# Early-fusion transformer layer: two patch embeddings moved ahead of the first scores, and the class row carried by the text transfer

## The reference

```python
# x (8, 3, 112, 112), txt (8, 128, 192)
patches = ...                                  # 49 patches of 16 x 16 x 3 = 768 numbers per image
embeds = einsum('bsp,pd->bsd', patches, W) + b + pos     # 49 rows of 192
h = concatenate([cls_embedding, embeds, txt])  # 1 + 49 + 128 = 178 rows per batch
# attention, 12 heads, queries and keys both xn * W_qk[head], values xn - mean(wte, axis=0)
xn = layernorm(layernorm(h)) * ln_w
out = softmax(causal(Q @ Q.T / sqrt(192))) @ (xn - avg_wte)
h = h + (out / position) @ W_o.T               # wte: 50257 x 192, read once for its mean
# 16 routed experts and one shared one, hidden size 128, then the residual
h = h + ffn(layernorm(h))
```

## Time and profile before

| | before |
|---|---|
| median of three executions | 447.61 us |
| lowest, highest | 445.42, 449.06 us |
| the profiled execution | 447.82 us |
| its span in the trace | 445.7 us |
| mean granted TensorE clock | 0.996 |
| TensorE busy | 434.3 us (97%) |
| VectorE busy | 277.3 us (62%) |
| ScalarE busy | 187.2 us (42%) |
| GpSimd busy | 68.3 us (15%) |
| DMA | 63.61 MB, mean 143 GB/s |

### The profile page before, as it was taken

The page is one execution under the profiler, slowest core; times in us unless marked ns, Lnnn a source line. Parts: engine busy times, 40 slices in busy tenths (PEclk is TensorE's granted clock), DMA queues, the critical chain, the costliest instruction groups (busy, mean ns, idle before and its releaser), DMA issues.

```text
span 445.7 us, 7188 instructions
## 1 busy us (share of the span) xinstructions
PE 434.3 (97%) x2572; PEld 378.3 (85%) x2572; DVE 277.3 (62%) x924; ACT 187.2 (42%) x565; POOL 68.3 (15%) x93
## 2 busy tenths in 40 slices
PE   8899999999999899999999999999999999999996
PEld 8687689877898667987779999999999999999995
DVE  5899865487654787447957855488553474433433
ACT  1766864447644466624532045633113412112111
POOL 4032122122212311210004114221002000000000
PEclk9999999999999999999989999999999999999999
DMA  5969999999999999997530052121332222322210
GB/s 175 295 245 211 213 213 213 213 213 215 213 214 213 214 213 213 214 214 190 209 121 2 1 220 76 50 67 49 89 91 63 63 69 60 97 68 69 64 42 35
DMA packets 20997, 63.61 MB, mean 143 GB/s; under 512 B 2572, under 2 KB 10836, under 8 KB 20578
## 3 DMA queue, kind: packets, MB, share of 16 engines
q0 software_dynamic: 7552, 39.39, 41.8%
q1 hardware_dynamic: 12546, 22.78, 17.3%
q10 hardware_dynamic: 864, 1.00, 0.7%
HBM read 61.88 MB, written 1.27 MB: 142 GB/s over the span
## 4 chain that ended last, share of the span: by engine, by line
PE 50%; DMA 44%; DVE 2%; issue 2%; SPq 1%; ACT 1%; POOL 1%; ACTq 0%; DVEq 0%
DMA area_w<-in_L_attn_wte_dram 39%; PE bank L927 15%; PE bank L898 5%; PE bank L897 5%; PE bank L895 5%; PE bank L896 5%; PE bank L894 5%; PE bank L810 3%; DMA woT<-in_L_attn_W_o_dram 3%; DMA lnw<-in_L_attn_ln_w_dram 1%; PE bank L757 1%; PE bank L921 1%; PE bank L783 1%; PE bank L748 1%; PE bank L782 1%
## 5 line engine op out<-in xcount | busy, mean ns | idle before, releaser
L810 PE MATMUL bank<-woT,area_o 128*128 128x192 f32 (+1 forms) x432 | 72.3, 327 | 0.0
L810 PEld LDWEIGHTS bank<-woT,area_o 128*128 128x128 f32 (+1 forms) x432 | 69.8, 182 | 0.6 <-issue 0.6
L521 ACT ACTIVATE pm<-pm,nmax 128x128 f32<-128x128 f32 x96 | 37.4, 390 | 72.9 <-DVE nmax L1031 72.9
L1128 DVE TENSOR_TENSOR area_b<-area_b,area_w 128x484 f32<-128x484 f32 (+1 forms) x36 | 24.1, 668 | 51.7 <-ACT area_b L594 50.4
L435 POOL DMA_DIRECT2D area_w<-in_L_attn_wte_dram x26 | 31.1, 1196 | 129.9 <-DMA area_w<-in_L_attn_wte_dram 129.9
L594 ACT ACTIVATE area_b<-bank,area_k 128x484 f32<-128x484 f32 (+1 forms) x24 | 15.8, 657 | 59.8 <-PE bank L898 59.8
L757 PE MATMUL bank<-pT,xn 128*128 128x356 f32 x96 | 39.7, 495 | 0.0
L544 ACT ACTIVATE area_b<-xb,w 64x192 f32<-64x192 f32 x96 | 38.1, 444 | 0.8
L894 PE MATMUL bank<-area_w_r,area_o_r 128*128 128x484 f32 (+1 forms) x84 | 37.4, 445 | 0.0
L927 PE MATMUL bank<-area_k,area_b 128*128 128x192 f32 (+1 forms) x192 | 35.3, 326 | 0.0
L927 PEld LDWEIGHTS bank<-area_k,area_b 128*128 128x128 f32 (+1 forms) x192 | 31.6, 182 | 0.9
(11 more groups left out here) (221 smaller groups left out, 916.6 us busy)
## 6 DMA issues: line engine op xcount, KB each, us to landing
area_w<-in_L_attn_wte_dram POOLq DMA_DIRECT2D x28, 1344.0 KB, 12.7
area_w<-gate_rows SPq DMA_DIRECT2D x24, 242.0 KB, 3.1
area_k<-in_experts_dram SPq DMA_DIRECT2D x8, 353.0 KB, 5.5
area_w<-gate_rows SPq DMA_DIRECT2D x12, 228.0 KB, 3.2
area_a<-in_experts_dram SPq DMA_DIRECT2D x6, 353.0 KB, 5.8
area_b<-gate_rows SPq DMA_DIRECT2D x8, 242.0 KB, 3.2
woT<-in_L_attn_W_o_dram SPq DMA_DIRECT2D x1, 1728.0 KB, 12.8
area_o<-in_x_dram SPq DMA_DIRECT2D x4, 384.0 KB, 5.8
```

Of the source, the lines that this page charges most:

```text
L521: act.activation(pm[:, sl, n, :], pm[:, sl, n, :], ACT.Exp, scale=-1.0, bias=nmax[:, sl, n:n + 1], accum_out=psums[:, sl, n:n + 1])
L810: last = pe.matmul(o, oT[:, c, at:at + n], woT[:, c, :], start=(c == 0), stop=(c == NCH - 1))
L1128: dve.tensor_tensor(sil[:, n % 2, 0:w], sil[:, n % 2, 0:w], wbc[m % RING][:, 0:w], ALU.mult).then_inc(weighted, 1)
```

## The change

- The class row is laid in DRAM ahead of each batch's text rows, so the text tensor has 129 rows. The first text transfer of each group then covers partitions 49 to 127, 79 rows, in place of 78. The transfer of the class row alone is gone, and VectorE's first wait is for 32 in place of 48.
- SP waits for the embedding weights alone (`s_tokw`) and then sends the patches of pairs 1 and 2; the wait for `s_small` comes behind them, and the one for `s_pos` is gone.
- `keep_awake(9)` becomes `keep_awake(2)` and `embed(1)`; `keep_awake(3)` ahead of the first scores becomes `embed(2)`. Both embeddings are gone from their later places.

```diff
--- before.py
+++ after.py
@@ -34,11 +34,12 @@
         self.n += 1
 
 
-def early_fusion_kernel(nc, x, txt, tok_W, tok_b, tok_pos, tok_cls, ln_w, W_qk, W_o, wte,
+def early_fusion_kernel(nc, x, txt, tok_W, tok_b, tok_pos, ln_w, W_qk, W_o, wte,
                         gate_w, gate_b, bias, experts, bdown, rows, out):
     PAIRS, _, KX, _ = x.shape
     B = 2 * PAIRS
     NTXT, _, E = txt.shape
+    NTXT -= 1
     NPOS = 49
     NIMG = 1 + NPOS
     S = NIMG + NTXT
@@ -320,22 +321,21 @@
             TM = P - NIMG
 
             def text_in(n, b0, b1):
-                sp.dma_start(hin[NIMG:P, b0:b1, 0, :], txt[0:TM, b0:b1, :]).then_inc(s_text[n], 16)
+                sp.dma_start(hin[NPOS:P, b0:b1, 0, :], txt[0:TM + 1, b0:b1, :]).then_inc(s_text[n], 16)
                 sp.wait_ge(s_zero, n + 1)
-                sp.dma_start(hin[0:TAIL, b0:b1, 1, :], txt[TM:NTXT, b0:b1, :]).then_inc(s_text[n], 16)
+                sp.dma_start(hin[0:TAIL, b0:b1, 1, :], txt[TM + 1:NTXT + 1, b0:b1, :]).then_inc(s_text[n], 16)
 
             sp.dma_start(ximg[:, 0], x[0]).then_inc(s_x[0], 16)
             text_in(0, 0, 2)
-            sp.dma_start(hin[NIMG - 1:NIMG, :, 0, :], tok_cls[0].rearrange("a (c e) -> a c e", c=1)
-                         .broadcast_to([1, B, E])).then_inc(s_text[0], 16)
-            sp.wait_ge(s_pos, 32)
+            sp.wait_ge(s_tokw, 16)
+            for i in range(1, 3):
+                sp.dma_start(ximg[:, i], x[i]).then_inc(s_x[i], 16)
             sp.wait_ge(s_small, 32)
-            sp.dma_start(ximg[:, 1], x[1]).then_inc(s_x[1], 16)
             text_in(1, 2, B)
-            for i in range(2, PAIRS):
+            for i in range(3, PAIRS):
                 sp.dma_start(ximg[:, i], x[i]).then_inc(s_x[i], 16)
             for k in range(2):
-                sp.dma_start(htail[TAIL * k:TAIL * k + TAIL, :, :], txt[TM:NTXT, k::2, :]).then_inc(s_text[1], 16)
+                sp.dma_start(htail[TAIL * k:TAIL * k + TAIL, :, :], txt[TM + 1:NTXT + 1, k::2, :]).then_inc(s_text[1], 16)
             sp.dma_start(woT[:], W_o).then_inc(s_wo, 16)
             sp.dma_start(gwa[:], gate_w[0:P, :]).then_inc(s_small2, 16)
             sp.dma_start(gwb[:], gate_w[P:2 * P, :]).then_inc(s_small2, 16)
@@ -672,7 +672,8 @@
             keep_awake(7)
             pe.wait_ge(s_tokw, 16)
             embed(0)
-            keep_awake(9)
+            keep_awake(2)
+            embed(1)
             pe.wait_ge(s_const, 1)
 
             def turn_in(b, bt, i):
@@ -812,12 +813,11 @@
                     last.then_inc(wo_done, 1)
 
             turn_in(0, 0, 0)
-            keep_awake(3)
+            embed(2)
             pe.wait_ge(s_pad, 1)
             queries_in(0, 0)
             scores(0, 0)
             turn_in(1, 1, 0)
-            embed(1)
 
             def mean():
 
@@ -848,8 +848,6 @@
                         project(i - 1, 2)
                     if u >= 1:
                         mix(u - 1, U + u - 1, i)
-                    if i == 0 and u == 0:
-                        embed(2)
                     if i == 0 and u == 1:
                         pe.wait_ge(xnT_ready, 4)
                         embed(3)
@@ -1170,7 +1168,7 @@
                 rows = slice(64 * half, 64 * half + NPOS)
                 return dve.tensor_tensor(hin[0:NPOS, half, 0, :], emb_bank[0][rows, 0:E], postab[rows, :], ALU.add)
 
-            dve.wait_ge(s_text[0], 48)
+            dve.wait_ge(s_text[0], 32)
             variance((1, 3), OPENING[0])
             dve.wait_ge(s_pos, 32)
             link(dve.tensor_tensor(postab[:], postab[:], tokb[:], ALU.add))
@@ -1387,7 +1385,7 @@
             finish(NG - 1)
 
 
-_INS = ['x', 'txt', 'L0_tok_W', 'L0_tok_b', 'L0_tok_positions', 'L0_tok_cls_embedding', 'L0_attn_ln_w', 'L0_attn_W_qk',
+_INS = ['x', 'txt', 'L0_tok_W', 'L0_tok_b', 'L0_tok_positions', 'L0_attn_ln_w', 'L0_attn_W_qk',
         'L0_attn_W_o', 'L0_attn_wte', 'L0_ffn_gate_w', 'L0_ffn_gate_b', 'L0_ffn_bias', 'experts', 'bdown']
 _OUTS = [((128, 12, 192), 'float32')]
 
@@ -1461,6 +1459,7 @@
     given = {name: _np.asarray(a) for name, a in inputs.items()}
     ffn = {name[len('L0_ffn_'):]: a for name, a in given.items() if name.startswith('L0_ffn_')}
     given['experts'] = _experts(*[ffn[n] for n in ('Wu', 'bu', 'Wg', 'bg', 'Wd', 'sWu', 'sbu', 'sWg', 'sbg', 'sWd')])
+    given['txt'] = _np.concatenate([_np.broadcast_to(given['L0_tok_cls_embedding'], (8, 1, 192)), given['txt']], axis=1)
     given['bdown'] = _np.zeros((P, 192), _np.float32)
     given['bdown'][0:17] = _np.concatenate([ffn['bd'], ffn['sbd'][None]])
     given['L0_ffn_gate_w'] = _np.concatenate([ffn['gate_w'], _np.zeros((64, 16), _np.float32)])
```

## The result

| | before | after |
|---|---|---|
| median of 5 runs | 446.82 us (445.42 to 449.06) | 462.59 us (460.78 to 463.22) |
| ratio, 95% interval | | 1.036 (1.033 to 1.039) |
| profiled execution, its span | 447.8, 445.7 us | 462.9, 460.9 us |

The changed kernel is slower by 3.6%. Between the two profiled executions lie 15.1 us, between the two spans 15.2 us. The forecast was 470 us in a range of 457 to 483.

A forecast was written before the change was run, and what follows sets the result against it. The prediction took the wte stream, started by woT's landing, as the bound. woT's delay, 4.2 + 18.8 - 2 = 21 us, plus 1 us for the clock, gave 447.8 + 21 + 1 = 469.8, so 470 us, range 457 to 483.

The forecast's parts named there:

- The bound is the stream that woT's landing starts: 28 back-to-back wte transfers, started by woT's landing, set the clock until 206 us; woT and stream end 21 us later.
- 79 rows go to one engine: 79 is prime, so one DMA engine carries all 158 and 474 text packets of the two groups; chance in order 0.84.
- Price of a packet, 43 ns: Time of one 768-byte text packet on its DMA engine, taken as 43 ns between bounds of 31.5 and 71.5.
- the forecast's 2.0 for contention: 2 us taken off woT's delay because the other DMA engines are out of work after some 22 us.
- How the delay comes about: SP's queue drains as before, and woT waits behind the text on the one engine, landing at about 46 us.
- First statistics at 14.4 with a wait of 8: VectorE's first statistics move from 7.92 to 14.4 us, behind the first group's text, with a wait of 8 us.
- TensorE's own path: The remaining text lands 13 us later, 15 with contention, less than the stream's 21; the six between are waited.
- One us for the clock: 1 us added for TensorE's lowered clock behind an idle stretch of several us before 227 us.
- Embeddings for zeros -0.7 us: Embeddings moved into the place of products of zeros take 0.7 us off TensorE's path.
- patches earlier -2.1 us: The second pair's patches are issued 2.1 us earlier, moving everything behind them on SP's queue, woT included, 2.1 us earlier.
- The first rival: The 79-row text is spread over many engines all the same; 446.1 us, 1.7 under the profiled execution, chance 0.11.
- The rival of woT not held: One engine carries the text but woT is served beside it, so only the text's landings count; 453.4 us, chance 0.05.

The follow-up runs named there:

- e1: The changed kernel with each 79-row text transfer cut into 1 and 78 rows; 445.5 us, ratio 0.998 to the kernel before.
- e4: The changed kernel with each 79-row text transfer cut into 15 and 64 rows; 445.6 us, ratio 0.997 to the kernel before.
- e5: The changed kernel with each 79-row text transfer cut into 5 and 74 rows; 451.5 us, ratio 1.013 to the kernel before.
- e6: The changed kernel with each 79-row text transfer cut into 3 and 76 rows; 447.3 us, ratio 1.002 to the kernel before.
- e12: The changed kernel, 79-row transfers kept, with woT issued ahead of the second group's text; 464.1 us, ratio 1.039 to the kernel before.
- e7: The changed kernel with 79 rows kept only in the first group, the second group's cut into 15 and 64; 451.3 us, ratio 1.014 to before.
- e8: The changed kernel with 79 rows kept only in the second group, the first group's cut into 15 and 64; 459.5 us, ratio 1.030 to before.
- e3: The kernel before with only the moved embeddings and SP's new order, class row still its own transfer, 78 text rows; 444.8 us, ratio 0.996.
- e9: e3 with GpSimd's rstd moved from behind the second to behind the fourth transfer of wte; 444.6 us, ratio 0.997 to the kernel before.
- e11: The kernel before with only SP's new order, embeddings and products of zeros in their old places; 444.3 us, ratio 0.997.
- e2: The kernel before with only the class row laid with the text (79-row transfers), embeddings and SP's order as before; 461.9 us, ratio 1.036.

## Why the prediction was right, step by step

- **The bound is the stream that woT's landing starts.** Right. Landing +15.4, sum +15.2, span +15.2. The end was reached through the last `rstd` in the stream's order (+16.2) and not through the last transfer.
- **79 rows go to one engine.** Right, and shown: 2914 packets, as forecast to the packet; a share of 0.07; e1, e4, e5 and e6 bring the time back in the order of the engine counts.
- **Price of a packet, 43 ns.** This is the term that was mis-sized. A lone engine took 34 ns. The 43 came from a stretch in which many engines worked at once, and it was worked out from the share, which makes 1.1 engines of a lone one: by the same way the lone engine has 0.070 x 16 x 5 us over 147 packets, 38 ns. So of the 9 ns too much about 4 lie in the way of counting and 5 in the crowded stretch. The lower bound, 31.5 ns, was nearer. e12's 86 ns is above the upper bound, but only while something else has the engine too.
- **The sum with 34 ns.** 146 x 0.034 = 5.0 for the first group, less 2.1 for the earlier issue, 438 x 0.034 = 14.9 for the second, less the forecast's 2.0 for contention, is 15.8, and 15.4 was measured. That it comes so close is partly luck, since the terms by themselves are off. By the stream's start all but the 79 rows brought 1.6 us (before to e4), the first group cost 3.7 (e7) and the second 13.7 (e8), and together they cost 0.4 less than that: -1.6 + 3.7 + 13.7 - 0.4 = 15.4. Each of these is one trace, and e3 and e9, with the same instructions on SP, start the stream at 21.44 and 23.22, so a term is known to 1 or 2 us only. The forecast also wasn't the same sum at its ends as in its middle: the sum with 31.5 ns takes off 2.4 for contention, the one with 71.5 ns nothing, and neither adds the 1 us for the clock.
- **How the delay comes about.** In part wrong. The prediction had SP issue everything on time, and woT wait on the slow engine behind the text. It was SP's issue of the next transfer that was held, for 17.22 us, and with it the patches, `htail` and woT for *all* engines. The sum came out alike because woT needs its last part either way. But the sign named for it (a share of 0.06 between 25 and 40 us) wasn't there: the share stood at 0.07 from 12 to 26.6 us, and from 28 to 40 it was 0.76, since what SP had been kept from issuing ran then on all engines.
- **First statistics at 14.4 with a wait of 8, from 43 ns a packet.** 13.12 and 6.97; with 34 ns the same sum gives 13.1.
- **TensorE's own path 13 to 15 us later, under the stream's 21.** It was 8.8, under 15.2. The order of the two was right, the sizes follow the packet price, and the difference of 6 was waited, as said. Of the two places named for the waiting, L1300 and `rs`, only the second was right: 0.78 us at the sum, not several, and 9.02 in one wait for `rs`.
- **One us for the clock.** It did not come. The forecast wanted an idle stretch of several us ahead of 227, and TensorE waited for nothing from 190 to 222 us. It did stand still for 4.46 us ahead of an embedding and for 6.69 ahead of the second row below, and its granted clock was lower behind both (0.62 from 14 to 16 us, 0.50 from 108 to 112), but both lie under the stream.

```profile
14.12 3.90 PE L664 MATMUL bank<-wtok,area_o 128*128 128x192 f32 x12 [4.46 <-DMA area_o<-in_x_dram]
...
109.20 1.12 PE L723 MATMUL bank<-ident,pm 128*128 128x128 f32 x4 [6.69 <-DVE pm L1038]
```

- **Embeddings for zeros -0.7 us, patches earlier -2.1 us.** The second is seen: e11 starts the stream at 21.85 instead of 25.17, 3.3 earlier, and has the sum 2.9 earlier; the medians are 1.6 apart (444.34 and 445.90). But in the change itself the 79 rows left little of it: 0.55 us between e2 and the change. The first rival, the text spread over many engines, was to be 1.7 us under the kernel before; e1 and e4, which spread it, are 1.0 and 0.9 under it. The 0.7 us isn't seen at all; e11 and e3 can't be told apart.
- **The rival of woT not held.** 453.4 us was its number. e12, which comes nearest to it, put woT ahead of the text and took 464.1: the rival counted the text's landing without what stands behind it on GpSimd, and without the sharing of the engine.

So the forecast (469.8 before rounding) was 7.2 us high in a sum whose bound and engine count held, while the way in which the delay comes about was wrong in part. 438 + 146 packets at 9 ns too much are 5.3 us, and the clock, which cost nothing, 1.0. The 34 ns sum is still 0.4 over what was measured, and the last half microsecond is between 447.8 + 15.4 = 463.2 and the median.

## What to carry to other kernels

Before adding a row to a transfer, look at what divides the new row count. One more row took a transfer from 13 engines to 1, and cutting the same bytes in two (1 + 78, 15 + 64) gave the whole loss back. The packet counts of a queue bear on the number of engines already in the trace before: what is left over after the data packets is the sum of the engines of its transfers, and two windows with different transfers in them, as the earlier trace rows, pin down the single ones. And when a transfer is made slow, ask what stands behind it in each order it is part of: here woT on SP's queue, and behind that, once woT was taken out of its way, the wte stream behind `rstd` on GpSimd.

## What the runs showed of the hardware

- One DMA engine alone took a 768-byte packet every 34 ns, 23 GB/s (147 packets in 5 us, the change); two engines took 118 in 2 us, 45 GB/s (e5). Beside the stream of wte the text got one packet through every 86 ns (81 in 7 us, e12).
- The issue that followed a one-engine transfer in the queue was held: 4.93 us behind 158 packets, 17.22, 15.71 and 14.96 us behind 474 (the change, e2, e8), 29.62 us where the engine was shared (e12), 5.66 behind a transfer on two engines (e5), 1.63 behind one on four (e6). Behind 78 rows on 13 engines it took 0.41 (e1). What in the queue holds it, no run shows. The prediction had no such term.
- TensorE's granted clock fell behind idle stretches of a few us. Behind 4.46 us of idle an embedding of twelve instructions took 3.90 us, and the windows over it have a granted clock of 0.62 and 0.53, near the lower of its two levels (0.5 is 1.2 of 2.4 GHz); from 18 us it is full again (third column from the right):

```profile
14.00:16.00 2.00, 1.88 (x7) 1.89 (x8) 1.78 (x10) 0.00 (x0) 0.96 (x2) 0.62 0.06 23
16.00:18.00 2.00, 2.00 (x8) 1.69 (x6) 1.83 (x7) 0.00 (x0) 0.31 (x1) 0.53 0.07 23
18.00:20.00 2.00, 2.00 (x13) 1.69 (x12) 1.47 (x5) 1.19 (x4) 0.55 (x1) 1.00 0.07 22
```

Behind 2.45 us in e4 and 6.26 us in e7 it took 3.88 and 4.21, and behind 1.74 us in e5 2.22, as when nothing was idle. In the change none of this reached the end, since it lay under the stream. In e4 and e7 it is in the chain: the wait for the patches and the slow embedding (11.30 to 15.18 us in e4, 15.32 to 19.53 in e7) stand ahead of `rstd` and of the third transfer of wte. So the removed products of zeros can cost something where the patches come late, though e4's median (445.6) shows no more than e1's (445.5), in which TensorE waited 0.50 us for them.
